# TensorE's arm of near samples written first and extended to the first energies, and both bias adds of the values behind the first row maximum

## The reference

```python
x = x + _L0_conv_ref(_gn(x), offset_w, offset_b, weight, bias)     # deformable 3x3 convolution
x = x + _L1_conv_ref(_gn(x), Wq, bq, Wk, bk, Wv, bv, Wo, bo)       # attention over 1024 positions
t = _to_tokens(x)
t = t + _L2_attn_ref(_ln_t(t), Wq, bq, Wk, bk, Wv, bv)             # attention with a log-distance bias
t = t + _L2_ffn_ref(_ln_t(t), gate_w, gate_b, W1, b1, W2, b2)      # 8 experts, the 2 best of each token
t = t + _L3_attn_ref(_ln_t(t), ...)                                # linear attention, 16 heads
t = t + _L3_ffn_ref(_ln_t(t), ...)                                 # 8 experts again
```

```python
acc = corner(y0, x0, (1 - ly) * (1 - lx)) + corner(y0, x0 + 1, (1 - ly) * lx) \
    + corner(y0 + 1, x0, ly * (1 - lx)) + corner(y0 + 1, x0 + 1, ly * lx)
out = jnp.einsum('bchwk,ock->bohw', sampled, weight.reshape(Oc, C, K * K))
```

## Time and profile before

| | |
|---|---|
| median of 3 runs (lowest, highest) | 2285.36 us (2282.35, 2286.89) |
| the profiled execution's own time | 2275.91 us |
| its span, first to last instruction | 2274.1 us |
| TensorE busy | 1854.9 us (82%) |
| VectorE busy | 1491.0 us (66%) |
| ScalarE busy | 1039.0 us (46%) |
| GpSimd busy | 571.8 us (25%) |
| mean granted clock of TensorE | 0.92 of 2.4 GHz |

### The profile page before, as it was taken

One profiled execution on the slowest core, in us unless ns is written; L12 is line 12 of the kernel. 1 busy time (PEld: TensorE's weight loads), 2 busy tenths in 40 slices (PEclk: granted clock), 3 DMA queues, 4 the chain that ended last, 5 costly groups with the idle time before them and its releaser, 6 DMA issues.

```text
span 2274.1 us, 36010 instructions
## 1 busy us (share of the span) xinstructions
PE 1854.9 (82%) x11024; PEld 1478.1 (65%) x11024; DVE 1491.0 (66%) x3473; ACT 1039.0 (46%) x1789; POOL 571.8 (25%) x535
## 2 busy tenths in 40 slices
PE   4778869796988879897888879897898878959749
PEld 1565748575867667675766667675766657746636
DVE  2357645777667866777667876677667865685463
ACT  3134226532755245832746245841746336624323
POOL 0000030314232413243231513243231423233030
PEclk8889989998999989998999989998999979979969
DMA  7910874176465845577455846588455846531500
GB/s 256 205 38 33 179 182 120 65 167 174 134 184 159 197 133 166 179 178 200 126 171 155 197 146 178 159 187 211 118 174 155 194 132 182 147 104 64 152 28 10
DMA packets 259913, 337.53 MB, mean 148 GB/s; under 512 B 29552, under 2 KB 191840, under 8 KB 259424
## 3 DMA queue, kind: packets, MB, share of 16 engines
q1 hardware_dynamic: 243648, 297.70, 49.2%
q0 software_dynamic: 14336, 29.39, 4.6%
q10 hardware_dynamic: 1696, 7.66, 0.9%
HBM read 267.56 MB, written 67.08 MB: 147 GB/s over the span
## 4 chain that ended last, share of the span: by engine, by line
PE 32%; issue 20%; DVE 17%; ACT 7%; DMA 6%; SPq 6%; POOL 5%; DVEq 4%; ACTq 2%; POOLq 0%
PE pair L951 5%; POOL gotten L811 4%; PE pair L1088 3%; DMA dist<-hats 3%; PE pair L1258 2%; PE pair L1248 2%; PE pair L938 2%; PE pair L1138 2%; DVE dist L1683 2%; ACT L1461 2%; SPq L603 2%; PE pair L1150 2%; ACT L1433 2%; PE pair L898 1%; ACT hidden_sb L1461 1%
## 5 line engine op out<-in xcount | busy, mean ns | idle before, releaser
L951 PE MATMUL pair<-dist,thirds 128*128 128x256 f32 (+6 forms) x1440 | 297.2, 358 | 86.4 <-issue 52.1
L951 PEld LDWEIGHTS pair<-dist,thirds 128*128 128x128 f32 x1440 | 258.3, 204 | 135.3 <-issue 74.2
L1088 PE MATMUL pair<-vt,dist 128*128 128x128 f32 x2048 | 264.8, 285 | 34.6 <-DVEq L1786 28.8
L1088 PEld LDWEIGHTS pair<-vt,dist 128*128 128x128 f32 x2048 | 250.4, 199 | 56.6 <-DVEq L1786 44.2
L811 POOL DMA_INDIRECT gotten<-ys,row x224 | 240.4, 1073 | 122.8 <-issue 65.8
L1461 ACT ACTIVATE hidden_sb<-pair,wring 128x128 f32<-128x128 f32 x644 | 184.8, 368 | 161.3 <-PE pair L1138 158.2
L1683 DVE TENSOR_TENSOR dist<-dist,prob 128x1024 f32<-128x1024 f32 x144 | 173.7, 1223 | 99.6 <-DMA prob<-hats 53.6
L1138 PE MATMUL pair<-turned_sb,wring 128*128 128x128 f32 x1288 | 190.6, 293 | 54.6 <-issue 22.7
L1138 PEld LDWEIGHTS pair<-turned_sb,wring 128*128 128x128 f32 x1288 | 170.8, 203 | 91.8 <-issue 36.2
L1792 DVE TENSOR_REDUCE nmax<-pair 128x1 f32<-128x1024 f32 x128 | 156.7, 1224 | 65.8 <-PE pair L1098 55.0
L799 POOL DMA_INDIRECT xs<-tnB,row x112 | 109.1, 974 | 325.5 <-DVEq L1973 293.0
(11 more groups left out here) (257 smaller groups left out, 3106.4 us busy)
## 6 DMA issues: line engine op xcount, KB each, us to landing
dist<-hats SPq DMA_DIRECT2D x576, 128.0 KB
wring<-wa SPq DMA_DIRECT2D x161, 321.0 KB, 3.6
wring<-wb SPq DMA_DIRECT2D x161, 321.0 KB, 3.8
prob<-hats SPq DMA_DIRECT2D x288, 128.0 KB, 3.6
hats<-dist SPq DMA_DIRECT2D x40, 512.0 KB, 3.8
ys<-by SPq DMA_DIRECT2D x70, 256.0 KB, 2.7
blocks_sb<-xs SPq DMA_DIRECT2D x28, 512.0 KB, 5.6
blocks_sb<-xs SPq DMA_DIRECT2D x14, 448.0 KB, 7.6
```

Source lines behind the costliest of these rows:

```text
L951: last = pe.matmul(pair[0][:, a:b], z[k // 3 % 2][:, c, k % 3, :], rhs(a, b), start=bank not in opened, stop=final, skip_group_check=True)
L1088: last = pe.matmul(psum[bank][:, 0:P], prT[j % 2][:, t, :], vt[:, t, :], start=(t == 0), stop=(t == NT - 1))
```

## The change

TensorE's `sampling` now takes all 18 halves before it reads the flag. The condition is turned round: the arm for near samples stands first. It holds the two drains that count for the far arm, and then the whole of `mid0` with its hooks (`projections`). The other arm holds the far samples and the same projections once more. `mid0` and its hooks are no longer called behind `sampling`. On VectorE both halves of the values get their bias in tile 0, behind the first row maximum. Nothing else is changed.

```diff
-LAST_HALVES = 10
...
-            def sampling(m, side):
+            def sampling(m, side, projections):
...
-                for n in range(LAST_HALVES):
+                for n in range(HALVES):
                     sampled_half(n)
                 pe.wait_ge(sem("far_known"), at(m, 1, 1))
                 flag = pe.value_load(isfar[0:1, 0:1], min_val=0, max_val=1)
                 before_arms = dict(uses)
-                with pe.If(flag > 0):
-                    for n in range(LAST_HALVES, HALVES):
-                        sampled_half(n)
+                with pe.If(flag < 1):
+                    pe.drain().then_inc(sem("far_used"), len(FAR))
+                    pe.drain().then_inc(sem("far_z_ready"), UNITS)
+                    projections()
                     after_arms = dict(uses)
+                with pe.Else():
+                    uses.update(before_arms)
                     for u, (k, c) in enumerate(FAR):
...
                         far_sample(k, c).then_inc(sem("far_used"), 1)
-                with pe.Else():
-                    uses.update(before_arms)
-                    for n in range(LAST_HALVES, HALVES):
-                        sampled_half(n)
+                    projections()
                     assert uses == after_arms
-                    pe.drain().then_inc(sem("far_used"), len(FAR))
-                    pe.drain().then_inc(sem("far_z_ready"), UNITS)
...
                 side = g_sides(m, p, rear, layer3, gating, nothing, nothing, experts)
+                g_side = side
+
+                def projections():
+                    for step in range(MID0_STEPS):
+                        mid0(m, step)
+                        g_side(CONV_HOOKS + step)
+
                 if front:
-                    sampling(m, side)
+                    sampling(m, side, projections)
                 else:
-                    for n in range(CONV_HOOKS):
+                    for n in range(G_HOOKS):
                         side(n)
-                for step in range(MID0_STEPS):
-                    if front:
-                        mid0(m, step)
-                    side(CONV_HOOKS + step)
...
-                    if a == 0 and j < 2:
-                        bank = SHARED[image(m), "v1", j]
-                        dve.wait_ge(sem("v1"), at(m, 2, j + 1))
-                        released(dve.tensor_tensor(vt[:, 4 * j:4 * j + 4, :], tiled(bank), over_tiles(const("bv1"), 4), ALU.add), bank)
-                        dve.drain().then_inc(sem("v1_kept"), 1)
+                    if a == 0 and j == 0:
+                        for h in range(2):
+                            bank = SHARED[image(m), "v1", h]
+                            dve.wait_ge(sem("v1"), at(m, 2, h + 1))
+                            released(dve.tensor_tensor(vt[:, 4 * h:4 * h + 4, :], tiled(bank), over_tiles(const("bv1"), 4), ALU.add), bank)
+                            dve.drain().then_inc(sem("v1_kept"), 1)
```

## The result

The changed kernel took 2254.64 us (median of four runs, 2252.26 to 2257.03), the kernel before 2283.86 beside it: a ratio of 0.9875, interval 0.9852 to 0.9898. On the scale of the median before, 2285.4 us, that is 2257; the forecast was 2261. So 28 to 29 us went where 24.5 were forecast. The span of the profiled execution went from 2274.1 to 2251.9 us, 22.2 less.

What follows compares the result with a forecast made beforehand. TensorE was taken as held up by code fetched behind the sampling's jump and by a bank VectorE freed late. -11.5 + 12 - 25 = -24.5 us from 2285.4 gave 2261 us, range 2243 to 2289.

Steps and rivals of the forecast that it cites:

- Edit 2: VectorE, first attention: both value biases behind the first row maximum free the bank earlier; 4.2 us in images 2 to 7, -25 us.
- Rival C: First attention: the bank's wait goes but the next takes its place, the bias move brings nothing; +0.5 us, 2286 us, chance 0.14.
- The new jump: TensorE, before the first energies: the jump over the far arm shows 1.5 us in each image, +12 us, bounds 4 and 58.
- 3.5 - 2.0 = 1.5: Before the first energies: jump of 3.5 us less the sequencer's lead of 2.0 leaves 1.5 us of idle TensorE an image.
- Rival A: Before the first energies: the jump keeps its 7.7 us, 5.7 show in each image, 46 us; 2295 us, slower, chance 0.13.
- Rival B: Before the first energies: the sequencer comes earlier, the whole jump hides under projections and values; -36.5 us, 2249 us, chance 0.15.
- The sampling, -11.5 us: TensorE's sampling: eight branches go, 3.8 + 3.9 us in images 0 and 1, less in 4 and 2; bounds 4 and 17.
- Edit 1: TensorE's near arm first, jump moved from the sampling to before the first energies: -11.5 + 12 = +0.5 us.
- The hint that the jump is moved and not removed: Skill page on instruction fetch: a far taken branch forces a DMA fetch wherever it stands, so the stall only moves.
- the marks of right: Signs such as 1 to 2.5 us idle at the new branch, 16 KB fetch within 1.5, VectorE's energy waits under 1.5.

Runs made afterwards that it cites:

- the runs with copies: Changed kernel plus unread memory copies beside TensorE's jump at the energies: two of 512 KB 2265.4 us, five 2271.9, two in 1 KB rows 2265.5.
- The later bias: Changed kernel with the values' second bias right behind the second row maximum instead of the first: 2257.7 us, ratio 0.9892.

## Why the prediction was right, step by step

1. **Edit 2, -25 us: right in size and place.** Alone it brought 26 us (0.9886 of 2279), and -25.9 to -26.6 in the first attention. It holds because TensorE, ScalarE and VectorE all waited in those 4 us: in images 2 to 7 ScalarE's wait in front of the first hidden activation was 5.7 to 6.1 us and is 1.0 to 2.7. Rival C, that the next wait takes it back, is refuted by that run. The later bias speaks for the bank: freed 4.61 us behind the start of the first row maximum instead of 3.47, it cost 0.89 us of wait.
2. **The new jump, +12 us: right.** 3.5 - 2.0 = 1.5 an image was the working; 3.30 to 4.22 less 2.14 (2.79 in two images) was measured, +11.5 and +11.6 in the third column. Rival A (7.7 us at the new place) did not come: that price belongs to the old place, where the run with the jump amid the sampling had it again. Rival B (hidden) is refuted by the 12.5 us of waits. Without the far arm 3.4 us of them are left.
3. **The reason given for 3.5 was only part of it.** I told the new place from the old by the DMA share, and load does lengthen the jump, by 1 to 2.5 us in the runs with copies. But in images 1 and 4 the share was as high as amid the sampling and the jump took 3.9 and 4.2 us. The value came from the nearest rows, jumps of SyncE and VectorE; that TensorE's comes out so near to it is in part luck.
4. **The sampling, -11.5 us: size not settled.** Seven profiled executions with the new sampling and the jump at the energies have -5.7 to -13.2 in the first column, mean -8.6. The shares by image are not settled either: image 0 gave 1.1 us of the 3.8 in the kernel after and 6.7 in its second execution. There VectorE waits 3.4 us for hats at every second half, and it did so before as well, but for one wait of 7.7 us behind the jump, which is gone. So in image 0 the hats' loads set the pace on both sides, and two executions of one kernel differ there by 5.6 us, more than the term. VectorE's row behind the jump before, and one of the rows after:

```profile
112.46 1.23 DVE L1683 TENSOR_TENSOR dist<-dist,prob 128x1024 f32<-128x1024 f32 x1 [7.74 <-DMA prob<-hats]
...
103.61 1.23 DVE L1683 TENSOR_TENSOR dist<-dist,prob 128x1024 f32<-128x1024 f32 x1 [3.42 <-DMA prob<-hats]
```

5. **Edit 1 in sum, +0.5 forecast; -1 to -9 by its own run.** With edit 2 there it makes no difference that can be told: 0.9875 and 0.9884 with it, 0.9886 without. The hint that the jump is moved and not removed was right: most of what the sampling got, the energies paid.
6. **What I would have called wrong** (5 us in front of the first energies, or none; sampling of images 0 and 1 as long as before; the first attention as long as before) did not come. Of the marks of right, two missed by little: one fetch of eight came 1.70 us behind its branch, not within 1.5, and VectorE's longest wait for energies was 1.84 us, not under 1.5. One mark would mislead: the profile calls the new idle time VectorE's, because VectorE's signal is the last one recorded, and the branch has none.

## What to carry to other kernels

A taken jump over a large arm has a price that depends on where it stands (here 3.3 to 9.3 us) and a cover that depends on what the sequencer has queued up by then (here 0.7 to 3.2 us): put it where queued work and a wait that the engine has anyway together are longer than the jump, and away from a burst of loads. Nothing that empties the engine (a drain) may stand between the queued work and the jump. Before such an edit, look whether a bank that another engine frees late is the larger wait: here one bias add, moved, brought nearly all of the gain.

## What the runs showed that was not expected

- A drain on TensorE's sequencer ahead of the jump cost all of its lead: 18.0 us in the second column with the drains, 6.9 and 7.3 with increments in their place.
- A far jump of TensorE is 2.3 to 3.3 us plus the time until its 16 KB packet starts. That was 0.9 to 1.3 us in the four images of the changed kernel where the DMA was quiet (share 0.08 or less up to the packet), 2.0 to 3.6 beside the copies, and 2.9 to 5.8 beside the hats.
- The unconditional branch to the very next instruction left no record of its own in the trace, so whether it was executed is open.
